# Block-diagonal products and the depthwise taps as 64x64 matmuls on quadrants of the array, in a new order of stages

## What is computed

```python
x = x + _L0_conv_ref(_ln_c(x), ...)      # 2-D DCT, 8x8 windows, channel attention, convolutions, inverse DCT
t = _to_tokens(x)
t = t + _L0_ffn_ref(_ln_t(t), ...)       # 8 experts of 64 -> 256 -> 64, the best two of a token are mixed
```

```python
q = _l2norm(split(x_tri @ Wq)); k = _l2norm(split(x_tri @ Wk)); v = split(x_tri @ Wv)
attn = softmax(einsum('bnhdm,bnhem->bnhde', q, k) * rescale)
x2 = (attn @ v as tokens) @ proj_w + proj_b                  # the low branch
h1 = g(depthwise3x3(g(conv1x1(x_dct)))); x_conv = h1 + x_dct  # the high branch, 3x3 taps per channel
x_high = g(conv1x1(x_conv)) + x_conv
x_out = coef * x_low + (1 - coef) * x_high + x_dct
```

## Time and profile before

| | us |
|---|---|
| median of three executions | 249.86 |
| the profiled execution, its own time | 248.42 |
| its span, first to last instruction | 246.4 |
| TensorE busy | 215.9 (88%), 1462 matmul records |
| VectorE busy | 153.3 (62%) |
| ScalarE busy | 128.6 (52%) |
| GpSimd busy | 47.0 (19%) |
| granted TensorE clock, mean of the span | 0.972 |
| DMA in the first three of 40 slices | 213 to 238 GB/s |

### The profile page before, as it was taken

How to read it: one execution, slowest core, us unless ns; L and a number is a source line. 1 busy time by engine, 2 the same in 40 slices (tenths; PEclk the granted TensorE clock), 3 DMA queues, 4 the chain that set the end, 5 groups by cost and what they waited for, 6 DMA issues and landing times.

```text
span 246.4 us, 3673 instructions
## 1 busy us (share of the span) xinstructions
PE 215.9 (88%) x1462; PEld 125.6 (51%) x1462; DVE 153.3 (62%) x266; ACT 128.6 (52%) x206; POOL 47.0 (19%) x44
## 2 busy tenths in 40 slices
PE   2588779999999965979299999999999999999993
PEld 2476569845755742969242244444444444444430
DVE  0696799997996998396996134444433334444445
ACT  2159731004508263155459676666667777666650
POOL 4670087003833058003210000000000000000000
PEclk9989999999999999999758999999999999999999
DMA  6992000000000000000000674326070714226001
GB/s 213 238 225 40 3 1 3 0 0 0 3 0 1 0 0 0 3 0 0 3 1 13 184 167 100 73 61 154 0 170 3 169 47 124 48 73 144 0 0 43
DMA packets 6592, 14.21 MB, mean 58 GB/s; under 512 B 2736, under 2 KB 4144, under 8 KB 5680
## 3 DMA queue, kind: packets, MB, share of 16 engines
q1 hardware_dynamic: 6576, 13.99, 23.9%
HBM read 12.81 MB, written 1.18 MB: 57 GB/s over the span
## 4 chain that ended last, share of the span: by engine, by line
PE 67%; DVE 18%; ACT 8%; DMA 2%; issue 2%; POOL 1%; SPq 0%; POOLq 0%; DVEq 0%
PE psum L626 23%; PE psum L642 22%; PE psum L484 6%; DVE place L916 4%; PE psum L456 3%; DVE place L994 3%; PE psum L466 3%; DMA sm<-in_small 2%; PE psum L554 2%; ACT place L740 2%; PE psum L563 1%; DVE place L993 1%; DVE st L903 1%; POOL place L837 1%; DVE st L887 1%
## 5 line engine op out<-in xcount | busy, mean ns | idle before, releaser
L626 PE MATMUL psum<-tok,w1s 128*64 128x512 f16 x512 | 61.9, 389 | 0.8 <-ACT w1f L789 0.4
L1088 DVE SCALAR_TENSOR_TENSOR term<-psum,sm,wide 128x512 f32<-128x512 f32 x32 | 24.0, 751 | 61.2 <-PE psum L642 60.5
L789 ACT ACTIVATE hid<-psum,b1p 128x512 f32<-128x512 f32 x64 | 38.6, 701 | 18.7 <-PE psum L626 18.6
L626 PEld LDWEIGHTS psum<-tok,w1s 128*64 128x64 f16 x512 | 28.8, 111 | 36.4 <-issue 8.9
L642 PE MATMUL psum<-hid,w 128*64 128x512 f32 x128 | 28.9, 593 | 0.0
L789 ACT ACTIVATE w1f<-psum,b1p 128x512 f32<-128x512 f32 x32 | 19.5, 688 | 15.2 <-PE psum L626 15.0
L1093 DVE TENSOR_TENSOR x<-x,term 128x512 f32<-128x512 f32 x32 | 22.2, 692 | 1.1
L789 ACT ACTIVATE w1g<-psum,b1p 128x512 f32<-128x512 f32 x32 | 19.6, 714 | 0.3
L642 PEld LDWEIGHTS psum<-hid,w 128*64 128x64 f32 x128 | 9.1, 137 | 15.0 <-issue 9.7
L916 DVE SCALAR_TENSOR_TENSOR place<-h_pad,sm,place 128x512 f32<-128x512 f32 x16 | 15.4, 965 | 0.6
L484 PE MATMUL psum<-h_pad,tap_bd 128*128 128x512 f32 x36 | 15.8, 592 | 0.0
(11 more groups left out here) (141 smaller groups left out, 322.9 us busy)
## 6 DMA issues: line engine op xcount, KB each, us to landing
wide<-gate_store SPq DMA_DIRECT2D x14, 512.0 KB, 6.3
xs<-in_x SPq DMA_DIRECT2D x2, 512.0 KB, 6.0
w1f<-in_W SPq DMA_DIRECT2D x2, 512.0 KB, 11.3
block_out<-x SPq DMA_DIRECT2D x4, 256.0 KB, 6.2
wide<-gate_store SPq DMA_DIRECT2D x2, 384.0 KB, 5.1
hid<-in_W1T SPq DMA_DIRECT2D x1, 512.0 KB, 12.5
w<-in_W SPq DMA_DIRECT2D x1, 512.0 KB, 13.7
c<-const SPq DMA_DIRECT2D x1, 483.5 KB, 4.3
```

Of the source, the lines that this page charges most:

```text
L626: mm = pe.matmul(h_bank(n)[side * H:(side + 1) * H, :], w1s[:, part, e, k * P + side * H:k * P + (side + 1) * H], tok[:, pair, half, b, :] ...
L789: act.activation(hid_of[u % 4][:, t, :], h_bank(n), ACT.Gelu, bias=b1p[:, e * KT + k:e * KT + k + 1]).then_inc(gelu_ready, 1)
L1088: dve.scalar_tensor_tensor(term[:, u % 2, :], y_bank(u), b2t[:, e:e + 1], gate_b[part][:, e % (E // 2), :], ALU.add, ALU.mult).then_inc(te ...
```

## The change

Products with block-diagonal or diagonal weights become matmuls over one quadrant of the array, 64 rows by 64 columns; a matmul's rows are the partitions that it reads, its columns those that it writes. The weights `wq_bd`, `proj_bd` and `tap_bd` shrink to 64 columns, the halves of the partitions being used apart. The first image of a pair (or four of eight window groups) goes through straight, rows 0 to 63 to columns 0 to 63 and rows 64 to 127 to columns 64 to 127; the second is crossed (`crossed`), so that its halves come out exchanged and a later stage exchanges them back. Thus four neighbouring matmuls use the four quadrants. This holds for `conv_in` (its edges are 128 rows by 64 columns), `gram_matrices`, `gram_times_w`, `norms`, `logits`, `taps`, `project` and `times_wv`; `low` uses the two straight quadrants. There are 428 matmuls ahead of the expert part before the change and 746 after it.

`first_taps` on VectorE is gone: `taps` makes both images' taps on TensorE, 36 matmuls a pair, after `norms_read` (VectorE has read the norms from the slot). Gram and mixing matrices are 64 columns wide, so that the two masks read 512 columns an operation. All of `TURN` is new. Among its numbers: `gram_matrices` of pair 0 comes before `conv_in` of pair 1, `biases` moves from 3 to 23 (behind `norm_tokens` of pair 1), `keep_gates` from (91, 101) to (101, 102). The constants grow by 128 columns, 64 KB.

```diff
-    "tanh_gap": (35, 92), "keep_gates": (91, 101),
+    "biases": (23, 23), "tanh_gap": (33, 91), "keep_gates": (101, 102),
...
+        def mix_index(g):
+
+            depth, column, odd = g // K, g % K // 2, g % 2
+            return column % 2 * K + depth * 4 + 2 * odd + column // 2
...
-        wq_bd = sb("wq_bd", [P, HEADS, P])
-        proj_bd = sb("proj_bd", [P, HEADS, P])
-        conv_bd = sb("conv_bd", [P, 4, P])
-        tap_bd = sb("tap_bd", [P, 9, P])
+        wq_bd = sb("wq_bd", [P, HEADS, H])
+        proj_bd = sb("proj_bd", [P, HEADS, H])
+        conv_bd = sb("conv_bd", [P, 3, P])
+        enter_bd = sb("enter_bd", [P, H])
+        tap_bd = sb("tap_bd", [P, 9, H])
...
+                for b in range(B2):
+                    for half in range(2):
+                        mm = pe.matmul(bank(slot(p, 1), b)[rows_of(crossed(half, b)), :], enter_bd[rows_of(half), :],
+                                       bank(xd[p], b)[rows_of(half), :], start=True, stop=True)
+                    mm.then_inc(c1a_done, 1)
+                edge = xd[p].rearrange("p (b n k) -> p b n k", b=B2, k=K)
+                for side in range(2):
+                    for b in range(B2):
+                        for half in range(2):
+                            mm = pe.matmul(bank(slot(p, 0), side)[rows_of(crossed(half, b)), b * H:(b + 1) * H],
+                                           conv_bd[:, side, rows_of(half)], edge[:, b, :, (K - 1) * (1 - side)], start=True, stop=True)
+                mm.then_inc(halo_done, 1)
...
             def gram_matrices(p):
...
+                pe.wait_ge(xt_ready, 2 * (p + 1))
+                for q in range(K):
+                    for half in range(2):
+                        for odd in range(2):
+                            v = xt[p][rows_of(odd), q * P + half * H:q * P + (half + 1) * H]
+                            mm = pe.matmul(bank(slot(p, 1), odd)[rows_of(half), q * H:(q + 1) * H], v, v, start=True, stop=True)
+                mm.then_inc(gram_done, 1)
...
-            def gram_times_w(p):
...
+                        for swapped in range(2):
+                            i = odd * K + swapped * 4 + q
+                            for half in range(2):
+                                mm = pe.matmul(bank(slot(p, odd), swapped)[rows_of(crossed(half, swapped)), q * P:(q + 1) * P],
+                                               gram[p][rows_of(half), i, :], wqk[rows_of(half), :], start=True, stop=True)
+                    mm.then_inc(t_done, 1)
...
             def norms(p):
...
-                columns = prod[p].rearrange("p g (d n) -> p d g n", d=DH)
+                columns = prod[p].rearrange("p (s g) (d n) -> p d s g n", s=2, d=DH)
+                side = G * HEADS
                 for d in range(DH):
-                    mm = pe.matmul(slot(p, 0)[:, 0:2 * G * HEADS], const("pick")[:, DH - 1 - d:DH - 1 - d + P], columns[:, d, :, :],
-                                   start=d == 0, stop=d == DH - 1)
+                    for swapped in range(2):
+                        for half in range(2):
+                            first = DH - 1 - d + half * H
+                            mm = pe.matmul(bank(slot(p, 0), swapped)[rows_of(crossed(half, swapped)), 0:side],
+                                           const("pick")[rows_of(half), first:first + H],
+                                           columns[rows_of(half), d, swapped], start=d == 0, stop=d == DH - 1)
                 mm.then_inc(norms_done, 1)
...
             def logits(p):
...
+                tk_of = tk[p].rearrange("p (h s n) -> p s h n", h=HEADS, s=2)
+                n = K * DH
                 for h in range(HEADS):
-                    mm = pe.matmul(slot(p, 1)[:, h * G * DH:(h + 1) * G * DH], wq_bd[:, h, :],
-                                   tk[p][:, h * G * DH:(h + 1) * G * DH], start=True, stop=True)
+                    for swapped in range(2):
+                        for half in range(2):
+                            mm = pe.matmul(bank(slot(p, 1), swapped)[rows_of(crossed(half, swapped)), h * n:(h + 1) * n],
+                                           wq_bd[rows_of(half), h, :], tk_of[rows_of(half), swapped, h],
+                                           start=True, stop=True)
                 mm.then_inc(logit_done, 1)
...
-            def second_taps(p):
-
-                pe.wait_ge(tk_ready, 2 * p + 1)
+            def taps(p):
+
+                pe.wait_ge(norms_read, p + 1)
                 pe.wait_ge(bd_ready, 1)
                 for tap in range(9):
-                    mm = pe.matmul(bank(slot(p, 0), 1), tap_bd[:, tap, :], shifted(p, 1, tap), start=tap == 0, stop=tap == 8)
-                mm.then_inc(second_taps_done, 1)
+                    for b in range(B2):
+                        for half in range(2):
+                            mm = pe.matmul(bank(slot(p, 0), b)[rows_of(crossed(half, b)), :], tap_bd[rows_of(half), tap, :],
+                                           shifted(p, b, tap)[rows_of(half)], start=tap == 0, stop=tap == 8)
+                        if tap == 8:
+                            mm.then_inc(taps_done, 1)
...
             def project(p):
...
+                    pe.wait_ge(attn_ready, 2 * p + swapped + 1)
+                    for h in range(HEADS):
+                        for half in range(2):
+                            mm = pe.matmul(bank(slot(p, 0), swapped)[rows_of(crossed(half, swapped)), h * n:(h + 1) * n],
+                                           proj_bd[rows_of(half), h, :],
+                                           bank(attn[p], swapped)[rows_of(half), h * n:(h + 1) * n], start=True, stop=True)
+                    mm.then_inc(y_done, 1)
...
             def times_wv(p):
...
+                    pe.wait_ge(yt_ready, 2 * p + swapped + 1)
+                    y_of = bank(y_t[p], swapped).rearrange("p (q f n) -> p f q n", f=2, n=H)
+                    for half in range(2):
+                        for odd in range(2):
+                            mm = pe.matmul(bank(slot(p, 0), odd)[rows_of(half), swapped * CHUNK // 2:(swapped + 1) * CHUNK // 2],
+                                           wv_rep[rows_of(odd), rows_of(half)], y_of[rows_of(odd), crossed(half, swapped)],
+                                           start=True, stop=True)
+                mm.then_inc(mix_done, 1)
...
             def low(p):
...
-                    mm = pe.matmul(slot(p, 0)[:, g * H:(g + 1) * H], mix[p][:, parity(g), :], xd[p][:, g * H:(g + 1) * H], start=True, stop=True)
+                    for half in range(2):
+                        mm = pe.matmul(slot(p, 1)[rows_of(half), g * H:(g + 1) * H], mix[p][rows_of(half), mix_index(g), :],
+                                       xd[p][rows_of(half), g * H:(g + 1) * H], start=True, stop=True)
...
             def gelu_depthwise(p):
-                act.wait_ge(first_taps_done, p + 1)
-                act.activation(bank(x_conv[p], 0), bank(x_conv[p], 0), ACT.Gelu).then_inc(dconv_ready, 1)
-
-            def gelu_second(p):
-                act.wait_ge(second_taps_done, p + 1)
-                act.activation(bank(x_conv[p], 1), bank(slot(p, 0), 1), ACT.Gelu).then_inc(second_dconv_ready, 1)
+                for b in range(B2):
+                    act.wait_ge(taps_done, 2 * p + b + 1)
+                    act.activation(bank(x_conv[p], b), bank(slot(p, 0), b), ACT.Gelu).then_inc(dconv_ready, 1)
...
-            def first_taps(p):
-
-                dve.wait_ge(halo_ready, p + 1)
-                dst = bank(x_conv[p], 0).rearrange("p (h k) -> p h k", k=K)
-                link(dve.tensor_scalar(dst, shifted(p, 0, 0), taps_w[:, 0:1], None, ALU.mult))
-                for tap in range(1, 9):
-                    last = dve.scalar_tensor_tensor(dst, shifted(p, 0, tap), taps_w[:, tap:tap + 1], dst, ALU.mult, ALU.add)
-                    if tap < 8:
-                        link(last)
-                last.then_inc(first_taps_done, 1)
...
             def mask_gram(p):
...
+                dve.wait_ge(gram_done, p + 1)
+                for odd in range(2):
+                    dve.tensor_tensor(gram[p][:, odd * K:(odd + 1) * K, :], split(bank(slot(p, 1), odd), H),
+                                      half_mask.unsqueeze(1).broadcast_to([P, K, H]), ALU.mult).then_inc(gram_ready, 1)
```

151 lines of the change are left out of this document (66 added, 85 removed).

## The result

| | kernel before | changed kernel |
|---|---|---|
| median, first comparison | 249.69 us (4 runs) | 240.75 us (4 runs) |
| ratio, with its 95% interval | | 0.9628 [0.9553, 0.9703] |
| median, second comparison | 249.97 us (11 runs) | 239.55 us (6 runs) |
| ratio, with its 95% interval | | 0.9572 [0.9520, 0.9623] |
| profiled execution, its own time / span | 248.42 / 246.4 us | 241.06 / 239.3 us |

Some executions are 1 to 2% slower at a lower granted clock; the ratios leave them out and the medians do not, so that the two differ in the third decimal.

What follows compares the result with a forecast made beforehand. Ahead of the first expert matmul TensorE and VectorE were both near their limit; after it TensorE alone. 246.4 - 6.7 + 2.1 = 241.8 us span, 243.8 as profiled, median 1.4 above: 245.2. Range 240 to 254.

Steps and rivals of the forecast that it cites:

- 25 ns for a record of 64 columns: TensorE's quadrant matmuls ahead of the experts: 25 ns a record of 64 columns, between bounds of 14 and 60 ns.
- faster records: Rival: quadrant records at 14 ns bring the first expert matmul 3.4 us sooner, 241.8 us; chance 0.17.
- the seam: Where the expert part begins: gates' copy 5.65 us later, so TensorE stands 2.0 us plus about 0.1 of signalling.
- places: TensorE stage ahead of pair 0's Gram matrices, laid at 1.9 us, the usual for 8 matmuls of 128 columns.
- the other paces: Taps of both images 7.7 to 8.0 us, W products 1.8 to 2.0, each mask operation 0.69 for 1.21.
- Column halves load and run at once: TensorE weight loads into different column halves overlap, as row halves do; otherwise about +1 us on the sum.
- the projection: TensorE's L509, 4.2 us before, would take 2.2 us at 28 ns a record, saving 2.0.
- VectorE's path: From the end of pair 1's norms to the end of mix_branches(1): 38.8 us, ending at 97.4 instead of 107.5.
- the biases cost nothing: Biases moved behind norm_tokens on VectorE delay pair 0's routing by 2.6 us, covered by its gates' later copy.
- no change: Rival: TensorE idles more ahead of the tokens, a second half-clock stretch between 97 and 107 adds about 5: 250; chance 0.15.
- the sum of 16.4 us saved on TensorE: Total of the TensorE savings ahead of the experts from quadrant matmuls; against it at most 2.2 us for shape changes.
- The laid path: New stage order laid on five queues with new durations: first expert matmul at 119.9 for 126.6, gain 6.7 us.

Runs made afterwards that it cites:

- e_norms2: Changed kernel with the 64 norms matmuls issued twice over for each pair; single execution 248.82 us.
- e_row_col: Changed kernel with norms on two quadrants by turns, same rows for pair 0, same columns for pair 1; single execution 242.74 us.
- e_both: Changed kernel with the gates' copy early and the biases early (both early moves); 236.26 us, 0.9444 of the kernel before.
- e_both2: e_both run a second time, same two early moves; 236.40 us, 0.9434 of the kernel before.
- e_warm: e_both plus ten idle matmuls where TensorE waits; 234.08 us, 0.9388 of the kernel before; 237.48 us in a single repeat execution.
- e_old_order: Changed kernel's quadrant matmuls and all taps on TensorE, stages in the order of the kernel before; 250.92 us, 1.0031 of the kernel before.
- e_one_diag: Changed kernel with norms on one quadrant at a time for pair 0, two diagonal quadrants by turns for pair 1; single execution 246.23 us.

## Why the prediction was right or wrong

**The step that failed: 25 ns for a record of 64 columns.** The sum had 25 ns, "the row nearest in size"; it is 14.6, the lower bound that the same paragraph had worked out (a quarter of half of 115). It is the pace within a row of records; e_norms2 shows that holes come on top. The router's records load 128 columns of weights each, so that their 25 ns are probably the load's; this was not tried. The norms took 2.08 us instead of 3.3, the Gram matrices 1.16 instead of 1.8. The rival "faster records" was the true one, with 0.17 of the chances. That its 241.8 us lies so near is partly luck: its gain was given back in part by the hole and by the seam, and 1.7 us came from where the profiled executions lie.

**A second mis-sized term: places.** "The usual one of TensorE with 8 matmuls of 128 columns being 1.9 us" does not hold for transposes, which leave one record each: places, 8 of them, took 1.02 us in the chain between its start and the next stage. The trace of the kernel before had it already (L435):

```profile
24.98 1.04 PE L435 MATMUL psum<-c,place 128*128 128x128 f32 x8
```

That is 0.9 us on the path of pair 0. Together: from W products(0) to the end of norms(1) 25.2 us were laid and 22.6 taken. Two norms at 1.2, Gram 0.6 and places 0.9 are 3.9 less; the hole of 1.24 us takes part of it back. W products began 1.1 us earlier than laid as well; places, windows and a Gram stage lie ahead of them, so the same two terms are in it, but how the 1.1 us divides was not worked out.

**Right: the other paces.** Taps 7.90 and 7.96 us (forecast 7.7 to 8.0), W products 1.98 and 2.12 (1.8 to 2.0), masks 0.683 us each. Column halves load and run at once, like row halves, now shown by e_row_col.

**A third term that fell out: the projection.** L509 at 4.2 us was to become 2.2 with 28 ns a record; L547 takes 4.2 us for its 64 records. In `project` the loop over straight and crossed stands outside, behind a wait for each half of the weights, so that only two quadrants work at a time. The logits, of the same form on all four, take 1.08 us for 32 records, the projection of pair 0 takes 2.08. The forecast's 2.0 us were not saved. The path lost little by it: in the chain L547 stands for 0.87 us (at 79.42).

**Right: VectorE's path.** From the end of norms(1) to the end of mix_branches(1) 38.8 us were laid; it took 38.86 (54.90 to 93.76). The match to 0.1 us is luck: two matmul stages in it ran partly at the lower clock. In the second execution of the kernel with both early moves, with the clock at 1.00 there, the same path takes 37.65 us (55.57 to 93.22), 1.2 less than laid.

**Right in kind: the seam.** TensorE stood 1.4 us behind VectorE's term at expert 3's down product, and the pair of down products took 1.7 us more than before (5.25 for 3.6); 2.1 were forecast. The whole seam, from the first expert matmul on, cost 2.7 (28.9 for 26.2), since the wait at gates_to_rows(0) below comes to it. The releaser was the term and behind it the gate load, as said:

```profile
136.10 0.75 DVE L1126 SCALAR_TENSOR_TENSOR term<-psum,sm,wide 128x512 f32<-128x512 f32 x1 [10.55 <-DMA wide<-gate_store]
...
139.61 0.75 DVE L1126 SCALAR_TENSOR_TENSOR term<-psum,sm,wide 128x512 f32<-128x512 f32 x1 [2.04 <-DMA wide<-gate_store]
...
140.42 1.94 PE L684 MATMUL psum<-w1g,w 128*64 128x512 f32 x8 [1.43 <-DVE term L1126]
```

**Wrong: the biases cost nothing.** "L626 waits for its tokens, not for them" overlooked that the biases hold up GpSimd, which makes those tokens (0.94 us), and "its gates' copy stands 5.65 us later in ScalarE's queue anyhow" overlooked that TensorE itself stands ahead of that copy, at gates_to_rows(0):

```profile
124.30 0.33 PE L647 MATMUL psum<-c,gates 128*128 128x128 f32 x1 [0.87 <-DVE gates L1093]
```

**The clock.** The "no change" rival came true in part. Half-clock stretches lay at 20 to 23 us and 88 to 90 us where there had been none, and they lengthened stages of that execution by 3.9 us in sum (conv_in(0) 0.9, dct_over_w(1) 1.4, to_frequencies(0) 0.4, low(1) 1.2). With both early moves one execution has both (e_both, 0.65 for 20 to 23 us and for 88 to 92) and the other neither (e_both2, 1.00 in both places), so they come and go by themselves; the stretch that the rival put between 97 and 107 us did not come.

**What the forecast did not see** is that matmuls and order only pay together. The laid path was right because it laid both; the sum of 16.4 us saved on TensorE said nothing, since the old order made none of it count.

## What to carry to other kernels

Block-diagonal weights of 64 columns cost a quarter on four quadrants, if neighbouring matmuls fall on different quadrants: half the data must be crossed, and the loop over quadrants must be the innermost. For 64 columns the 14.6 ns hold for a row of some hundred records; beyond that count the holes in. In this kernel the relieved TensorE gave nothing until the order let the pairs run one stage apart, so matmuls and order are to be searched together and judged together. VectorE work that reads both inputs from SBUF is to be kept away from GpSimd's long operations, in both directions: either can wait for the whole of the other's.

## What was not expected of the hardware

Holes in a dense stream. In both traces of the changed kernel TensorE stands still 10 records into logits(0), for 0.7 and 1.24 us, with nothing that it waits for. Where five idle matmuls (ten records) lie ahead of that place (e_warm), the hole comes ten records sooner, between norms and logits:

```profile
35.66 2.08 PE L503 MATMUL psum<-wide,c 64*64 64x64 f32 x128
39.10 1.10 PE L517 MATMUL psum<-place,wq_bd 64*64 64x128 f32 x32 [1.37 <-issue]
```

So its place is a count of instructions and no stage: both traces of the changed kernel and those of e_both2, e_warm and e_norms2 have 474 matmul records ahead of the first hole. In e_norms2 there are three; between the first two lie exactly 128 records (116 and 2 of norms, 10 of logits), before the third 382, or some three times 128, as a few records can be missing. In e_old_order two such holes (0.29 and 0.77 us) are 128 records apart as well. At half the pace (e_row_col) and at a quarter (e_one_diag) there is none: logits followed norms at once, and in e_row_col twice the norms' time (3.76 for 2.08) put the taps back by only 0.1 to 0.6 us. The stretches of the changed kernel show small transfers beside it, 8 GB/s in 2 us, or 16 KB, and the page counts 16 packets of 16 KB for instructions (11 before). Such transfers also lie where there is no hole, as at 42 to 44 us:

```profile
36.00:38.00 2.00, 1.89 (x129) 1.92 (x133) 0.00 (x0) 0.95 (x2) 1.59 (x1) 1.00 0.00 0
38.00:40.00 2.00, 1.53 (x89) 1.28 (x80) 0.72 (x3) 0.00 (x0) 0.00 (x0) 1.00 0.04 8
40.00:42.00 2.00, 1.23 (x30) 1.08 (x34) 1.79 (x7) 0.00 (x0) 0.00 (x0) 1.00 0.00 0
```

```profile
q8 instruction: 16, 0.26, 0.4%
```

It looks as if small matmuls are used up faster than their instructions are loaded, in blocks of 128 records and their 128 weight loads, so that 14.6 ns holds only for a hundred records or two in a row. The place and the spacing are shown; that the cause is the loading is argued from these rows, and no run isolated it.

An operation of VectorE that reads both inputs from SBUF and one of GpSimd held each other up for their whole length: 3.98, 2.26 and 4.43 us for a 0.75 us operation, beside GpSimd's 3.98, 2.23 and 4.38. Not every operation did: in the changed kernel the reduction L1004 (one input) took its usual 0.69 us at 60.66, while GpSimd's L886 ran from 60.12 to 62.49, and L992, which reads PSUM, its usual 1.21 at 65.75 beside L889.
